# Even expert tiles gathered by quarter rows and turned by VectorE instead of TensorE

## The reference

```python
gate_scores = xf @ gate_W + gate_b
topk_scores, topk_idx = jax.lax.top_k(gate_scores, 2)
weights = jax.nn.softmax(topk_scores, axis=-1)
def expert(w1, bb1, gg1, bbe1, w2, bb2, gg2, bbe2):
    h = relu(_layernorm(xf @ w1 + bb1, gg1, bbe1))
    return _layernorm(h @ w2 + bb2, gg2, bbe2)
out = sum over the two chosen experts of weight * expert(xf); result = out + xf
```

## Time and profile before

| | |
|---|---|
| median of three runs | 1171.98 us (1170.48 to 1174.3) |
| the profiled execution | 1170.26 us, of which the traced span is 1168.5 us and 1.8 us lie around it |
| TensorE matmul busy | 1108.3 us, 95% of the span |
| VectorE busy | 910.5 us, 78% |
| ScalarE busy | 722.2 us, 62% |
| GpSimd busy | 393.4 us, 34% |
| mean granted TensorE clock | 0.991 of 2.4 GHz |

### The profile page before, as it was taken

One profiled execution on the slowest core, in us unless ns is written; L12 is line 12 of the kernel. 1 busy time (PEld: TensorE's weight loads), 2 busy tenths in 40 slices (PEclk: granted clock), 3 DMA queues, 4 the chain that ended last, 5 costly groups with the idle time before them and its releaser, 6 DMA issues.

```text
span 1168.5 us, 24237 instructions
## 1 busy us (share of the span) xinstructions
PE 1108.3 (95%) x6017; PEld 905.0 (77%) x6018; DVE 910.5 (78%) x2172; ACT 722.2 (62%) x2148; POOL 393.4 (34%) x328
## 2 busy tenths in 40 slices
PE   6999999999989999999999888999999999999993
PEld 5888888888877787777777666777888888888882
DVE  6888888887874778878878877877777777777774
ACT  5223332233377777768676644866787787877873
POOL 3000000000034433545536364445534434443432
PEclk9999999999999999999999998999999999999998
DMA  8544545445340133143143377786555454444543
GB/s 261 163 149 159 190 148 173 151 163 207 126 147 1 57 89 111 56 124 100 46 145 90 128 206 219 201 249 152 94 85 81 81 85 80 86 81 81 88 63 40
DMA packets 95316, 144.76 MB, mean 124 GB/s; under 512 B 20864, under 2 KB 37428, under 8 KB 94607
## 3 DMA queue, kind: packets, MB, share of 16 engines
q1 hardware_dynamic: 77338, 106.83, 28.8%
q0 software_dynamic: 17216, 35.73, 17.4%
q10 hardware_dynamic: 693, 1.36, 0.4%
HBM read 82.69 MB, written 64.76 MB: 126 GB/s over the span
## 4 chain that ended last, share of the span: by engine, by line
PE 72%; DVE 9%; issue 7%; DMA 6%; ACT 3%; POOL 2%; DVEq 0%; POOLq 0%; ACTq 0%; SPq 0%
PE banks L1126 27%; PE banks L716 17%; PE banks L928 7%; PE banks L781 6%; DMA out<-rows,scatter_rows 4%; PE banks L893 3%; PE banks L906 3%; PE banks L1154 2%; PE banks L1138 2%; ACT rows L1335 2%; DVE operands L1615 2%; PE banks L917 1%; PE banks L754 1%; DVE rows L1917 1%; ACT operands L1218 1%
## 5 line engine op out<-in xcount | busy, mean ns | idle before, releaser
L1126 PE MATMUL banks<-operands 128*128 x1608 | 390.5, 398 | 9.2 <-ACT operands L1218 5.0
L1126 PEld LDWEIGHTS banks<-operands 128*128 128x128 f32 x1608 | 299.5, 190 | 73.9 <-issue 14.2
L716 PE MATMUL banks<-operands 128*128 128x512 f32 (+2 forms) x1224 | 290.1, 393 | 3.6 <-DVE operands L1615 3.6
L716 PEld LDWEIGHTS banks<-operands 128*128 128x128 f32 (+1 forms) x1224 | 226.1, 192 | 48.3 <-DVE operands L1615 3.7
L1218 ACT ACTIVATE operands<-banks 128x512 fp32r<-128x512 f32 (+1 forms) x232 | 137.6, 602 | 63.4 <-PE banks L807 34.2
L1615 DVE TENSOR_TENSOR operands<-banks,operands 128x512 fp32r<-128x512 f32 (+1 forms) x232 | 156.7, 683 | 15.6 <-ACT operands L1218 12.2
L1335 ACT ACTIVATE rows<-banks,score_shift 128x77 f32<-128x77 f32 x512 | 158.4, 337 | 11.2 <-DVE score_shift L1839 10.9
L2686 POOL DMA_INDIRECT out<-rows,scatter_rows x67 | 106.4, 1588 | 155.3 <-DVE rows L2419 109.7
L1218 ACT ACTIVATE operands<-rows 128x512 fp32r<-128x512 f32 (+2 forms) x77 | 54.0, 710 | 163.6 <-DVE rows L1686 139.4
L1540 ACT ACTIVATE banks<-banks,param_cols 128x128 f32<-128x128 f32 x268 | 99.2, 431 | 82.2 <-PE banks L1154 75.6
L2357 DVE BATCH_NORM_STATS2 moe_stats<-banks 128x6 f32<-128x512 f32 x134 | 93.2, 696 | 37.5 <-PE banks L1126 31.5
(11 more groups left out here) (191 smaller groups left out, 1603.1 us busy)
## 6 DMA issues: line engine op xcount, KB each, us to landing
expert_parts<-operands SPq DMA_DIRECT2D x32, 512.0 KB, 3.0
operands<-expert_parts SPq DMA_DIRECT2D x8, 2048.0 KB, 11.4
rows<-in_x SPq DMA_DIRECT2D x8, 1024.0 KB, 5.5
rows<-in_L_ffn_W SPq DMA_DIRECT2D x32, 256.0 KB, 3.6
x_rows<-rows SPq DMA_DIRECT2D x8, 1024.0 KB, 4.3
rows<-x_rows SPq DMA_DIRECT2D x8, 1024.0 KB, 6.2
xf_rows<-rows SPq DMA_DIRECT2D x32, 256.0 KB
out<-rows SPq DMA_DIRECT2D x32, 256.0 KB
```

The lines of the kernel that those rows point to most:

```text
L716: last = nc.tensor.matmul(dst, stationary(a, k), moving(b, k), start=(t == 0 and k == 0), stop=(t == len(terms) - 1 and k == n_k - 1))
L1126: last = nc.tensor.matmul(dst, stationary[:, a, k, :], weights[:, w, bass.ds(e, 1), a2, k, :].rearrange("p e f -> p (e f)"), start=False, ...
```

## The change

- `load_slots`: for every even tile from 14 on, SyncE issues four more small DMAs, one for each 32 partitions, which lay the same 128 entries out as 32 x 4 (`square_slots`). Partition 32 q + r holds places 4 r to 4 r + 3, for each quarter q.
- `gather_rows`: for these tiles VectorE makes a 128 x 4 index, 4 * token + q.
- `gather`: for these tiles GpSimd issues four gathers instead of one. Each takes 128 quarter rows (512 bytes) by one column of the index. All go to `xg[0]`, whose earlier rows must have been turned.
- `turn_rows`: a new VectorE instruction at the head of an odd step i turns the 128 x 512 floats of tile i+3 in squares of 32 x 32. It waits for all four gathers. TensorE's `rows_in` of that tile (4 transposes) goes.
- `rows_hi` and `rows_lo` of these tiles read the turned rows in SBUF (`xq_turned`) with a step of 32 floats, no longer a PSUM bank.
- The order of the features changes for all tiles: block k of the product takes features 4 p + k. So `W1` is loaded as "(p k) f", and TensorE's `rows_in` of the other tiles reads `xg` with a step of 4 floats.
- ScalarE's `deviations` stands behind the high part of the hidden features in odd steps, no longer ahead of it. The semaphore `cx_done` is split by parity.

```diff
             def load_slots(n, u):
                 sp.dma_start(tile_slots[:, bass.ds(i, 1), :]...).then_inc(slots_in[u], 16)
+                if in_squares(n, u):
+                    for q in range(KC):
+                        sp.dma_start(square_slots[q * SQ:(q + 1) * SQ, bass.ds(n - SQUARES_N, 1)]...,
+                            slots_d[bass.ds(row, P), :].rearrange("(r b) w -> r (b w)", r=SQ)).then_inc(slots_in[u], 16)
...
             def rows_in(n, u):
-                    last = nc.tensor.transpose(cx_bank[u][:, k * P:(k + 1) * P], xg[u][:, k * P:(k + 1) * P], ident[:, :])
-                last.then_inc(cx_done, 1)
+                    last = nc.tensor.transpose(cx_bank[u][:, k * P:(k + 1) * P],
+                                               xg[u].rearrange("p (f k) -> p k f", k=KC)[:, k], ident[:, :])
+                last.then_inc(cx_done[u], 1)
...
-                if after >= 3:
+                if after >= 3 and not in_squares(n + 1 + u, 1 - u):
                     rows_in(n + 1 + u, 1 - u)
...
+            def turn_rows(n):
+                dve.wait_ge(gathered[0], gathers(n + 1, 0))
+                need(dve, cx_lo, 2 * n - 1)
+                V.transpose(xq_turned.rearrange("p (k b r) -> p b k r", k=KC, r=SQ), xq_rows).then_inc(cx_done[0], 1)
+
+            def rows_lo(n, u):
+                if in_squares(n, u):
+                    lo_part(xT[:, LO].rearrange("p k (r b) -> p k r b", r=SQ), xq_features,
+                            xT[:, HI].rearrange("p k (r b) -> p k r b", r=SQ)).then_inc(cx_lo, 1)
...
             def gather_rows(n, u):
+                if in_squares(n, u):
+                    V.scalar_tensor_tensor(
+                        gix_squares, square_slots[:, bass.ds(n - SQUARES_N, 1), :, 0].rearrange("p n b -> p (n b)"),
+                        float(KC), quarter, ALU.mult, ALU.add).then_inc(gix_ready, 1)
+                    return
...
             def c_tile(n, u, coming, after):
+                if after >= 3 and in_squares(n + 1 + u, 1 - u):
+                    turn_rows(n + 1 + u)
...
             def gather(n, u):
-                need(pool, cx_done, i - 1)
-                need(pool, gathered[u], 16 * n)
+                need(pool, cx_done[u], n)
+                need(pool, gathered[u], gathers(n, u))
                 need_alone(pool, gix_ready, i + 1, pool_passed)
+                if in_squares(n, u):
+                    for b in range(P // SQ):
+                        G.indirect_dma_start(xg[0][:, b * P:(b + 1) * P], None, xf_quarters,
+                                             bass.IndirectOffsetOnAxis(gix_squares[:, b:b + 1], 0)).then_inc(
+                            gathered[u], 16)
+                    return
```

More of the change, by code:

```diff
@@ L301, in decoder_layer @@
         late_in, late_hi, late_lo = sems("late_in late_hi late_lo")
+        cx_done = [sem(f"cx_done{i}") for i in range(2)]
         gathered = [sem(f"gathered{i}") for i in range(2)]
@@ L442, in decoder_layer, with in_squares, gathers, slot_loads @@
         block = ctx.enter_context(nc.Block())
+        def in_squares(n, u):
+            return u == 0 and (not isinstance(n, int) or n >= SQUARES_N)
+        def gathers(n, u):
+            return 16 * (P // SQ * n - (P // SQ - 1) * SQUARES_N) if in_squares(n, u) else 16 * n
+        def slot_loads(n, u):
+            return 16 * ((KC + 1) * n - KC * SQUARES_N) if in_squares(n, u) else 16 * n
         def split_source(n):
@@ L1531, in deviations, with hidden @@
                 nc.scalar.activation(c_ve[:, which], c_mv[:, which, 1], ACT.Sqrt, bias=eps[:, 0:1]).then_inc(c_dev, 1)
-            def hidden(i, e, after=None):
+            def hidden(i, e, after=None, behind=False):
                 if after == 1:
@@ L1542, in hidden @@
                                          bias=pcol[:, bass.ds(e * KC + (ROW_BE1 + k), 1)]).then_inc(relu_done, 1)
-                if after is not None and after >= 2:
+                if after is not None and after >= 2 and not behind:
                     deviations(i, True, True)
@@ L1547, in hidden @@
                 hi_part(hTc[:, HI].rearrange("p k t -> p (k t)"), ch_bank).then_inc(hh_ready, 1)
+                if after is not None and after >= 2 and behind:
+                    deviations(i, True, True)
                 if after is not None and after < 2:
@@ L1574, in c_tile @@
                 if early >= 2:
-                    hidden(i, experts[2], after)
+                    hidden(i, experts[2], after, in_squares(n + 1 + u, 1 - u))
                 if early == 1:
```

69 lines of the change are left out of this document (43 added, 26 removed).

## The result

The changed kernel takes 1227.95 us (median of 4 runs, 1217.34 to 1248.32) beside 1173.14 us before on the same chip; the ratio is 1.043 with a 95% interval of 1.033 to 1.052. On a second chip, under the name a0_after, it took 1232.99 us beside 1171.51, ratio 1.053 (1.050 to 1.056). The forecast was 1183.0 us with a range of 1168 to 1200: the sign was right, the size was not, +12.7 us against +55 to +61. The profile shown here is that of a0_after, span 1230.4 us.

A forecast was written before the change was run, and what follows sets the result against it. TensorE bound the kernel before; GpSimd's serial chain, 12.86 us a pair against TensorE's new 12.26, was to bind it after, ending the last adds 12.7 us late: 1170.26 + 12.7 = 1183.0 us, range 1168 to 1200.

The forecast's parts named there:

- Part 1, TensorE's saving: TensorE loses four row transposes in each of 27 even tiles, 0.44 us each, 11.9 us in all; stepped reads taken as free.
- a GpSimd that doesn't bind: Rival: quarter gathers cost less or adds land sooner, so VectorE holds the pair at 12.35 us; 1160.8 us, chance 0.14.
- Part 2, VectorE: VectorE gains the turn, 681 ns, and stepped reads taken as free: 12.35 us a pair, a tenth over TensorE's 12.26.
- the high end: Upper price of VectorE's stepped reads in turn and low part: 1.20 us more, 13.55 us in a pair.
- a rival: Slow reads with a step make VectorE's pair 13.55 us against GpSimd's 12.86; 1194 us, chance 0.17.
- Part 3, GpSimd's chain: Four gathers, 5.2 us for 1.3, make GpSimd's serial chain 5.75 + 7.1 = 12.86 us a pair, so it binds.
- Part 4, SyncE: Four extra slot loads per tile cost nothing; weight loads move some 14 us later, slower adds up to 7 us, taken as nothing.

The follow-up runs named there:

- f3_two_and_two: The changed kernel with its four quarter gathers split, two in the odd step and two at the head of the even step; 1191.32 us, ratio 1.017.
- k2_two_and_two_plain: The changed kernel with gathers split two and two between steps and no read with a step (feature and token order left out); 1192.03 us, ratio 1.017.
- b1: The changed kernel with TensorE's row transposes of 40 tiles reading contiguously, without the step of 16 bytes; 1237.25 us, ratio 1.055.
- c1: The changed kernel with the turn, high and low parts of the 27 turned tiles reading contiguously; 1251.95 us, ratio 1.072.
- d1: The changed kernel with no read with a step left, in TensorE's transposes or in the turned tiles; 1253.15 us, ratio 1.070.
- k5_pause_behind: The kernel before with three extra quarter gathers for each even tile from 14 on, then three small GpSimd fills ahead of the add; 1217.57 us, ratio 1.040.
- e3_three_and_one: The changed kernel with the fourth quarter gather moved from the odd step to the head of GpSimd's next even step; 1245.26 us, ratio 1.058.
- l2_three_one_pause: e3_three_and_one with two small GpSimd fills ahead of the add of each odd step; 1199.93 us, ratio 1.023.
- k1_two_extra: The kernel before with two extra quarter gathers behind the row gather of each even tile from 14 on; 1203.36 us, ratio 1.027.
- f2_extra_odd: The kernel before with three extra quarter gathers behind the row gather of each odd tile from 15 on; 1264.4 us, ratio 1.078.
- k4_pause_between: The kernel before with three extra quarter gathers for each even tile from 14 on, a small GpSimd fill ahead of each; 1262.96 us, ratio 1.073.
- f4_extra_direct: The kernel before with three extra plain 64 KB copies by GpSimd, without indices, for each even tile from 14 on; 1169.65 us, ratio 0.998.

## Why the prediction was wrong

- **Part 1, TensorE's saving: right.** e1_one_gather, which keeps the change but for three gathers and the reads with a step, takes 1163.3 us; the forecast for a GpSimd that doesn't bind was 1160.8. The row transposes with a step cost 207 instead of 140 ns in each weight load; f3_two_and_two has them and k2_two_and_two_plain has not, and both stand at 1.017.
- **Part 2, VectorE: the wrong end, without effect.** I took the reads with a step as free, since the nearest rows were those of the same operations without it. They cost 0.41 and 0.38 us in a pair, 0.79 of the 1.20 that I had as the high end, and ScalarE's 0.53. By the rule of the page "SBUF — State Buffer" of the Trainium skill, section "Door 1: The DMA port swizzle", they had to be slow, and the trace agrees. As a rival it was priced at 1194 us by way of VectorE's pair; that step failed, for b1, c1 and d1 against a0_after, and k2 against f3_two_and_two, show no gain from the removal of the steps.
- **Part 3, GpSimd's chain: right in each leg, wrong as the bound.** The legs are 7.48 and 5.83 us against 7.1 and 5.75 in the rows above, and five pairs up to 931.25 us take 13.06 each; where the chain is all there is, in k5_pause_behind, the time is 2.6 us from what the same prices give. (Six adds at 5.7 us from 1138.4 end at 1172.6, not 1172.5; nothing hangs on it.) But the step "a pair costs GpSimd 5.75 + 7.1 = 12.86 us, that is more than 12.26" took issuing as something that only GpSimd pays for. The forecast had no term for a run of indirect DMAs with which TensorE's signals come late. The runs showed it in its place: three more gathers alone make the kernel before 106 us slower, where the chain by itself was put at 1178 to 1190 us, 5 to 17 over before (e2_extra_gathers). The earlier trace rows could not show it: at most three indirect DMAs stand together there at gaps of 0.3 us, and then comes the wait for a landing. In the steady part of before an add stands off from the gather by a wait of 1.9 us for `y2` (72.9 us in 38 waits between 850 and 1120 us), and that gap is what the change took away in odd steps.
- **What that term is worth.** From 936 us on the signal is 1.4 to 4.0 us later than 0.85 once in a pair, at a point with nothing to cover it: ScalarE's relu, then its high part, then TensorE's second product. TensorE idles, is granted the lower clock for part of the stretch (0.93 to 0.95 on average from 900 to 1110 us), and the 17 pairs from 931.25 to 1194.15 us take 15.46 us each instead of 12.86. That is 44 of the 49 us by which the span of 1230.4 us lies over the 1181.2 of the forecast. VectorE's index and with it the next run come late as well, which may be what keeps the run at the same place in each pair, so that the pattern feeds itself; this is my reading, no run tests it. e3_three_and_one shows that shortening GpSimd's chain doesn't break the pattern, k5_pause_behind and l2_three_one_pause that a pause ahead of the add does.
- **Part 4, SyncE: right.** The four extra loads of each even tile ended at 989 us, and no engine waited for one (no wait for L670 in the list of waits; e1_one_gather has them all). The weight loads of the last pair moved from 769.58 to 786.41 us, 17 us where 14 were forecast, and e1_one_gather, which has all of them, is 2.5 us from the time forecast without that cost.
- **The range** ended at 1200 because every bound in it was one of durations and landings. Nothing in it stood for a new interaction, though the change put a pattern on GpSimd that the expert part of before never had: up to nine indirect DMAs at gaps of 0.3 us (from 809.07 us on: add, four gathers, scatter, add, row gather, scatter), and at least the four gathers and the add in every pair. Before, the longest run is four scatters and a gather at 699.85 us, with no add in it. e2_extra_gathers, one edit, would have shown it.

What stays open is the mechanism. The rows show TensorE's signal late by 0 to 4 us, and where: from about the third or fourth of a run of indirect DMAs until the run ends. In e2_extra_gathers, k1_two_extra, f2_extra_odd and k4_pause_between the relu mostly starts 0.5 to 0.9 us after the end of the add's issue, but in the changed kernel at 1006.80, before that end at 1007.47. The moment at which TensorE's transposes meet the run counts for much: in a0_after they start 4.13 and 4.20 us after the first DMA of the run at 922.71 and 909.85 us and the delay is 1.48 and 1.46 us; at 935.58 they start 4.33 us after it, and the delay is 4.85. No run holds that moment fixed and changes only the count, the kind or the pause, so each of these three is bound up with it. Whether the transposes themselves run late or only their signal does can't be told for certain, since the ends of matmuls are modelled in the profile; but TensorE's next transposes and the first product start at 1004.17 and 1004.57, 0.44 and 0.84 us behind those of 1003.73, which speaks for the signal.

## What to carry to other kernels

Look at the longest run of indirect DMAs that GpSimd issues without a wait, in the trace and after the change: one that goes from three to four or more, with the last of them an add to memory, may cost other engines far more than GpSimd's own time. If it must be, split the run between steps (f3_two_and_two), or let the add stand off from the gathers, even by idle work: with 1.31 us in l2_three_one_pause and 1.67 in k5_pause_behind the delay was back at 0.85 us in nearly every pair, with 0.8 us in f3_two_and_two it was still about 0.6 us more. Which moment of the run the other engines' signals meet was not held fixed in these runs, so read the distance from producer to consumer again after each such edit. And where an edit multiplies a kind of instruction, measure the kernel before with only these instructions added; here that one run shows the loss that no sum had in it.

## What the runs showed of the hardware

- An indirect DMA of 128 rows mostly takes GpSimd 0.94 to 1.02 us to issue, whether rows of 512 B or 2 KB, and 0.3 us pass to the next; an add of 128 rows of 2 KB takes 1.6 us. Three plain copies of 128 rows of 512 B took 1.73 to 1.80 us together (f4_extra_direct). A quarter gather that started while VectorE's subtraction out of SBUF ran took up to 1.66 us (a0_after).
- The granted clock of TensorE falls with the longer of these stalls: 1.00 between 900 and 1040 us where the signals are in time (e1_one_gather, k5_pause_behind) and also where they are late by 1.3 to 1.8 us (k1_two_extra), 0.90 to 0.95 where they are late by 1.1 to 3.3 us (d1_plain_both, e2_extra_gathers).
- A 32x32 turn of 128x512 that reads with a step of 16 B takes 1091 ns, contiguous 701; a subtraction out of SBUF with a step of 128 B 1067 against 658; ScalarE's copy with that step 1157 against 624; a 128x128 weight load with a step of 16 B 207 against 140.
